# Two half-width units at the front, an interleaved end, and a second per-sample sum on the activation engine

## The chip, the cores and the metric

The kernel runs on one core of one Trainium2 chip. The core has a matrix engine (PE, its weight loads shown apart as PEld), a vector engine (DVE), an activation engine (ACT), a general engine (POOL), and a queue engine (SP) that mostly issues transfers. Sixteen DMA engines move the data. The metric is the device time of one execution in microseconds (us); lower is better. A "profiled execution" is one run recorded by the hardware profiler; its rows are what is read here.

## The reference

A recommendation model's interaction tower, 1024 samples, 32 embedding fields of 16 numbers, three interaction layers of 64 outputs, then a dense tower:

```python
B, M, D, LAYERS = 1024, 32, 16, [64, 64, 64]
e = jnp.stack([tbl_f[ids[:, f]] for f in range(32)], axis=1)      # (B, M, D)
x0 = e; xk = x0; outs = []
for W in (W0, W1, W2):                                            # (M, h, 64)
    xk = relu(einsum('bmd,bhd,mhk->bkd', x0, xk, W))
    outs.append(sum(xk, axis=2))                                  # over d
z = concatenate(outs, axis=1)                                     # (B, 192)
h = concatenate([z, dense_ctx], axis=1)                           # (B, 208)
h = maximum(h @ W_top1 + b_top1, 0)                               # 512
h = maximum(h @ W_top2 + b_top2, 0)                               # 256
y = h @ W_top3                                                    # (B, 1)
```

Everything is 32-bit float. Per sample and per d, a layer is the outer product of the 32 fields with the layer's input, contracted with a weight matrix. The sum over d of each layer's output is what "the sums" mean below.

## The kernel before

**Units.** The samples are worked on in 16 units of 64. The free axis of a tile holds one unit's samples and d values, N = 64 x 16 = 1024 columns, in two halves (blk) of 512. Layers 2 and 3 contract 32 x 64 = 2048 pairs, 16 tiles of 128 partitions; layer 1 uses symmetry and takes 4 tiles and one small tile of squares.

**How a unit gets its data.** POOL gathers the rows of a unit from the tables with 16 indirect transfers (line 295), 64 samples times two groups of fields on 128 partitions. DVE transposes them (`turn`, line 331) into xt, 8 transfers (`store`, line 205) write them to a scratch tensor in HBM three times over, and SP loads them back spread over partitions: `first` (line 226, 0.5 MB, for x0) and four groups of four tiles (`load_group`, line 231, 2 MB each) into a ring of 6 buffers.

**What computes.** DVE multiplies tiles by the layer's input (x0, x1 or x2, in PSUM) into prod, a ring of 12 tiles (`multiply`, line 341), in steps of 1, 2 or 4 tiles. POOL makes 3 of 16 tiles of layers 2 and 3 (tiles 5, 6, 7; line 307) from copies x1_pool and x2_pool. PE contracts each tile with its weights, one matmul for each half of the columns, into the PSUM bank acc (`contract`, line 484; a matmul shows as two records in the profile, so a tile is four records). ACT evicts acc with a relu into x1 or x2 (line 392, four pieces), into the POOL copy (four more), and into relu_out (`keep`, line 407), from which the sum over d is taken into z.

**The sums.** For layers 1 and 2 DVE takes one reduction (`sum_d`, line 353). For layer 3 ACT does it (`sum_3`, line 400): 32 small activations with an accumulator output, each recorded as an ACTIVATE and a READ_ACCUMULATOR.

**Order.** Nothing is scheduled by a tool; each engine's list is written by hand and the semaphores tie them together. PE takes layer 2 of unit u, layer 1 of u+1, layer 3 of u. DVE takes the same order; inside layer 3 of u it sums layer 2 after step 2 and turns unit u+2 before step 3, and after layer 3 it sums layer 1 of u+1. ACT's list per unit: x0 of u+1 (`base_tile`, line 413), squares of u+1 (line 419), x2 of u (`after_2`), x1 of u+1 (`after_1`), relu_out of layer 3 of u (`after_3`), its sum. SP's list: the stores of u+1, `first`, groups 0 and 1, then group 2 once DVE made step 0 of layer 3 of u, group 3 once it made step 1 and POOL its third tile.

**The end.** For the last unit there is no next layer 1 to put between layer 2 and layer 3. Then the dense tower runs for all samples at once, 512 columns per matmul (lines 542 and 546 for the first matrix, 553, 559), with ACT evictions (lines 471, 475, 478), and two output transfers (line 285).

## Time and profile before

| | |
|---|---|
| median of 3 runs | 680.73 us (674.42 to 684.67) |
| the profiled execution | 675.9 us, of which 674.0 us is the span of the trace |
| TensorE clock, mean granted | 0.967 of full speed |
| busy: PE, DVE, ACT, POOL | 85%, 83%, 47%, 68% |
| HBM | 227 GB/s mean over the span |

Time stamps are us from the span's start. A row of the timeline reads: start, length, engine, line, operation, written <- read, shapes, count; in brackets the idle time of the engine ahead of it and what ended that. The row of a group merges neighbouring instructions and shows the form of the first.

### The profile page before, as it was taken

The page shows a single profiled execution, that of the slowest core. Times are in us where ns is not written, and L with a number is a line of the kernel's source. Part 1 is how long each engine was busy: PE and PEld are TensorE (multiplying, and loading weights), DVE is VectorE, ACT ScalarE, POOL GpSimd, SP SyncE. Part 2 cuts the span into 40 slices and gives each one's busy share as a digit, 9 for nine tenths or more (in the row PEclk, how much of TensorE's full clock was granted, in tenths as well). Part 3 has the DMA queues.
Part 4 walks back from the last instruction along what each step waited for, and adds up shares of the span by engine and source line. Part 5 has one row for each costly group of instructions (what it writes and reads, how often), then busy time and mean ns, then how long its engine had stood idle before and what let it go on. Part 6 is the DMA issues. An engine that isn't in the chain of part 4 may idle for free.

```text
span 674.0 us, 7501 instructions
## 1 busy us (share of the span) xinstructions
PE 572.9 (85%) x2472; PEld 191.5 (28%) x2472; DVE 558.0 (83%) x231; ACT 317.5 (47%) x1311; POOL 461.0 (68%) x353
## 2 busy tenths in 40 slices
PE   0047599989989898989898989898998989895997
PEld 0002132333323232323232323232333423231332
DVE  0039798989999999999899999999998999996400
ACT  0031447364555646454646473746456464643031
POOL 5776484977878887878697979788887873443000
PEclk9998699899999899989999999999898999997999
DMA  3296685776757576767586777777685667570000
GB/s 91 65 353 218 261 300 230 271 286 254 298 223 298 223 248 253 255 256 283 214 301 241 276 282 273 285 270 287 244 311 201 248 241 309 206 243 0 1 0 0
DMA packets 32918, 153.35 MB, mean 228 GB/s; under 512 B 11600, under 2 KB 21584, under 8 KB 24816
## 3 DMA queue, kind: packets, MB, share of 16 engines
q1 hardware_dynamic: 22656, 149.31, 57.6%
q0 software_dynamic: 8192, 2.11, 2.6%
q10 hardware_dynamic: 2032, 1.46, 0.7%
q8 instruction: 19, 0.31, 0.2%
q14 instruction: 19, 0.16, 0.1%
HBM read 147.61 MB, written 5.25 MB: 227 GB/s over the span
## 4 chain that ended last, share of the span: by engine, by line
PE 52%; DVE 21%; DMA 11%; issue 6%; ACT 5%; SPq 3%; POOL 2%; ACTq 0%; DVEq 0%
PE acc L484 47%; DVE prod L341 19%; DMA spread<-x_scratch 6%; DMA x_scratch<-xt 4%; ACT x L392 4%; SPq L205 3%; POOL rows L295 2%; PE x L553 2%; PE x L542 1%; DVE z L353 1%; DVE xt L331 1%; DMA first<-x_scratch 1%; PE x L559 1%; PE x L546 0%; PE acc L542 0%
## 5 line engine op out<-in xcount | busy, mean ns | idle before, releaser
L341 DVE TENSOR_TENSOR prod<-spread,x 128x4096 f32<-128x4096 f32 (+2 forms) x179 | 531.1, 3022 | 47.7 <-ACT x L392 20.4
L484 PE MATMUL acc<-prod,w 128*64 128x512 f32 x1932 | 453.7, 617 | 95.1 <-DVE prod L341 89.5
L295 POOL DMA_INDIRECT rows<-table,idx x256 | 242.7, 948 | 79.0 <-issue 70.4
L307 POOL TENSOR_TENSOR prod_pool<-spread,x_pool 128x1024 f32<-128x1024 f32 x93 | 218.1, 2374 | 84.3 <-ACT x_pool L392 84.1
L484 PEld LDWEIGHTS acc<-prod,w 128*64 128x64 f32 x1932 | 147.8, 141 | 389.5 <-issue 351.7
L392 ACT ACTIVATE x<-acc 64x512 f32<-64x512 f32 x128 | 73.0, 570 | 79.0 <-PE acc L484 77.8
L407 ACT ACTIVATE relu_out<-acc 128x512 f32<-128x512 f32 x48 | 28.7, 597 | 157.3 <-PE acc L484 156.5
L400 ACT ACTIVATE relu_out<-relu_out 128x16 f32<-128x16 f32 x480 | 95.3, 200 | 0.5
L484 PE MATMUL acc<-prod_pool,w 128*64 128x512 f32 x372 | 90.9, 592 | 0.0
L400 ACT ACTIVATION_READ_ACCUMULATOR relu_out<-relu_out 128x1 f32 x480 | 89.8, 187 | 0.0
L392 ACT ACTIVATE x_pool<-acc 64x512 f32<-64x512 f32 x128 | 75.7, 591 | 1.9
L484 PEld LDWEIGHTS acc<-prod_pool,w 128*64 128x64 f32 x372 | 28.4, 137 | 51.4 <-issue 49.7
L419 ACT ACTIVATE square<-spread 32x1024 f32<-32x1024 f32 x16 | 16.9, 1056 | 39.7 <-DMA spread<-x_scratch 39.7
L353 DVE TENSOR_REDUCE z<-relu_out 128x32 f32<-128x512 f32 x33 | 22.2, 674 | 5.8 <-ACT relu_out L407 5.8
L413 ACT ACTIVATE x<-first 128x1024 f32<-128x1024 f32 x16 | 16.4, 1028 | 20.3 <-DMA first<-x_scratch 19.9
L331 DVE STREAM_TRANSPOSE xt<-rows 128x256 f32<-128x256 f32 x16 | 10.6, 661 | 15.1 <-DMA rows<-table,idx 15.1
L484 PE MATMUL acc<-square,w_sq 32*64 32x512 f32 x64 | 17.2, 613 | 0.0
L553 PE MATMUL x<-prod,spread 128*128 128x512 f32 x32 | 14.0, 594 | 0.9 <-ACT prod L471 0.9
L413 ACT ACT_TABLE_LOAD x1 | 1.3, 1283 | 28.3 <-issue 28.3
L542 PE MATMUL x<-z,spread 64*128 64x512 f32 x36 | 8.5, 606 | 1.5 <-DVE z L353 1.5
L553 PEld LDWEIGHTS x<-prod,spread 128*128 128x128 f32 x32 | 6.0, 190 | 8.8 <-issue 8.8
L471 ACT ACTIVATE prod<-x,b 128x512 f32<-128x512 f32 x6 | 3.8, 683 | 9.9 <-PE x L546 9.9
(20 smaller groups left out, 26.9 us busy)
## 6 DMA issues: line engine op xcount, KB each, us to landing
spread<-x_scratch SPq DMA_DIRECT2D x63, 2048.0 KB, 9.3
first<-x_scratch SPq DMA_DIRECT2D x16, 512.0 KB
rows<-table,idx POOLq DMA_INDIRECT x256
x_scratch<-xt SPq DMA_DIRECT2D x64, 48.0 KB
spread<-x_scratch SPq DMA_DIRECT2D x4, 512.0 KB, 8.2
x_scratch<-xt SPq DMA_DIRECT2D x60, 32.0 KB
w<-w ACTq DMA_DIRECT2D x2, 512.0 KB, 5.7
spread<-wt SPq DMA_DIRECT2D x2, 384.0 KB, 4.4
```

Source lines behind the costliest of these rows:

```text
L205: engine.dma_start(to, src.to_broadcast([J, times, BLK // 2])).then_inc(scratch_in[u % 2], 16)
L295: nc.gpsimd.indirect_dma_start(rows[u % 2][:, j * D:(j + 1) * D], None, table, bass.IndirectOffsetOnAxis(ap=idx[:, u, j:j + 1], axis=0)).t ...
L307: nc.gpsimd.tensor_tensor(prod_pool[:, k % POOL_SLOTS, :], tiles(u, t, 1)[:, 0, :], x[:, :], ALU.mult).then_inc(pool_ready, 1)
L331: nc.vector.transpose(xt[u % 2][:, :].rearrange("p (b e) -> p e b", e=D // 2), rows[u % 2][:, :].rearrange("p (j e c) -> p e c j", e=D // ...
L341: nc.vector.tensor_tensor(prod[:, at:at + count, :], tiles(u, t, count), x[:, :].rearrange("p (a n) -> p a n", a=1).to_broadcast([P, count ...
L353: nc.vector.tensor_reduce(z[:, layer, u * 32:(u + 1) * 32], relu_out[layer][:, :].rearrange("p (e b d) -> p b e d", e=2, d=D // 2), axis=m ...
L392: last = nc.scalar.activation(to[K * half:K * half + K, blk * BLK:(blk + 1) * BLK], src[K * blk:K * blk + K, :], ACT.Relu)
L400: last = nc.scalar.activation(kept[:, b, :, :], kept[:, b, :, :], ACT.Copy, accum_out=z[:, 2, u * 32 + b:u * 32 + b + 1])
L407: nc.scalar.activation(relu_out[layer][:, :], src[:, :], ACT.Relu).then_inc(relu_ready[layer], 1)
L413: nc.scalar.activation(x0[:, :], first[:, :], ACT.Copy).then_inc(x0_ready, 1)
L484: last = nc.tensor.matmul(to[K * blk:K * blk + K, :], w, moving[:, blk * BLK:(blk + 1) * BLK], start=start, stop=stop)
L553: last = nc.tensor.matmul(to_h2(t, g), w_top2[:, s, t * P:(t + 1) * P], h_1[:, s, g, :], start=s == 0, stop=s == H1 // P - 1)
```

## The change

Four edits come together.

1. **Half units.** The first 64 samples are worked on as two units of 32 (u = 0 and 1), each with half as many columns (512) and with its rows on four groups of fields, so that 8 indirect transfers gather a unit. Then come 15 units of 64; in all there are 17 units, and the last has the number LAST = 16. A half unit's scratch is written by 10 transfers of its own (`store_half`), half of them by ACT for unit 0. Layer 3 of unit 0 and layer 2 of unit 1 are all made by DVE. The ids come laid out by the host, in two transfers. An activation on one element (`warm`) is placed ahead of ACT's first wait on the transposed rows.
2. **Interleaved end.** Of layer 3 of unit 15, steps 0 and 1 and the POOL tiles are taken first, then layer 2 of unit 16, then the rest of layer 3 of unit 15, then layer 3 of unit 16, whose input x2 is written to the place of x0. PSUM banks come from a table (BANKS).
3. **Sums of layer 1.** From unit 1 on ACT makes them with the 32 small activations, right after `after_1`; DVE keeps that of unit 0 alone.
4. **Tower.** The 64 samples of the half units have z of 128 partitions (the two halves of d) instead of 64, so the first matrix takes 480 columns in the old way and 2 x 32 columns in matmuls of their own. There are four output transfers.

```diff
+HALVES = 2
+UNITS = HALVES + (B - HALVES * S // 2) // S
+LAST = UNITS - 1
+FULL = (UNITS - HALVES) * S // 2
+COLS = FULL + HALVES * S // 2
...
-    return () if (layer, u) == (2, 0) else (5, 6, 7)
+    return () if (layer, u) in ((2, 0), (3, 0), (2, 1)) else (5, 6, 7)
...
+CUT = 2
+CUT_ORDER = ([("step", 0), ("step", 1), ("pool", 0), ("pool", 1), ("pool", 2)], [("step", 2), ("step", 3)])
+
+
+def sequence():
+
+    def every(layer, u):
+        return [(layer, u, i) for i in range(len(steps_of(layer, u)))]
+
+    yield from every(1, 0)
+    for u in range(LAST):
+        yield from every(2, u)
+        yield from every(1, u + 1)
+        if u + 1 < LAST:
+            yield from every(3, u)
+    yield from every(3, LAST - 1)[:CUT]
+    yield from every(2, LAST)
+    yield from every(3, LAST - 1)[CUT:]
+    yield from every(3, LAST)
...
+        def store_half(engine, u, f):
+            for copy in range(copies(u, f)):
+                to = scratch(u, J // 2 * f + M * copy)
+                to = bass.AP(tensor=to.tensor, offset=to.offset, ap=[[N // 8, 4], [N // 2, J // 2], [1, N // 8]])
+                engine.dma_start(to, xt[u % 2][32 * f:32 * f + 32, 0:N // 8]).then_inc(scratch_in[u % 2], 16)
...
             turn(0)
             layer_1(0)
-            for u in range(UNITS):
+            turn(1)
+            for u in range(LAST):
                 dve.wait_ge(x_ready[0], u + 1)
                 for i in range(len(steps_of(2, u))):
                     multiply(2, u, i, x1)
-                    if u == 0 and i == 2:
-                        turn(1)
                 if u == 0:
                     sum_d(0, 0)
-                if u + 1 < UNITS:
-                    layer_1(u + 1)
+                layer_1(u + 1)
                 dve.wait_ge(x_ready[1], u + 1)
-                for i in range(len(steps_of(3, u))):
-                    if i == 3 and u + 2 < UNITS:
-                        turn(u + 2)
-                    multiply(3, u, i, x2)
-                    if i == 2:
-                        sum_d(u, 1)
-                if u + 1 < UNITS:
-                    sum_d(u + 1, 0)
-            sum_d(UNITS - 1, 2)
+                if u + 1 < LAST:
+                    for i in range(len(steps_of(3, u))):
+                        if i == (1 if u == 0 else 3) and u + 2 < UNITS:
+                            turn(u + 2)
+                        multiply(3, u, i, x2)
+                        if i == 2:
+                            sum_d(u, 1)
+            for i in range(CUT):
+                multiply(3, LAST - 1, i, x2)
+            sum_d(LAST - 1, 1)
+            dve.wait_ge(x_ready[0], LAST + 1)
+            for i in range(len(steps_of(2, LAST))):
+                multiply(2, LAST, i, x1)
+            for i in range(CUT, len(steps_of(3, LAST - 1))):
+                multiply(3, LAST - 1, i, x2)
+            dve.wait_ge(x_ready[1], LAST + 1)
+            for i in range(len(steps_of(3, LAST))):
+                multiply(3, LAST, i, x2_of(LAST))
+                if i == 1:
+                    sum_d(LAST, 1)
+            sum_d(LAST, 2)
...
-            def sum_3(u):
-                act.wait_ge(relu_ready[2], u + 1)
-                kept = relu_out[2][:, :].rearrange("p (e b d) -> p b e d", e=2, d=D // 2)
+            def sum_d(u, layer):
+                act.wait_ge(relu_ready[layer], u + 1)
+                kept = relu_out[layer][:, 0:width(u) // 2].rearrange("p (c b e) -> p b c e", c=2, b=S // 2)
                 for b in range(S // 2):
                     last = nc.scalar.activation(kept[:, b, :, :], kept[:, b, :, :], ACT.Copy,
-                                                accum_out=z[:, 2, u * 32 + b:u * 32 + b + 1])
-                last.then_inc(summed[2], 1)
+                                                accum_out=z[:, layer, z_at(u) + b:z_at(u) + b + 1])
+                last.then_inc(summed[layer], 1)
...
+            act.wait_ge(consts_in, 48)
+            nc.scalar.activation(warm[:, :], w_sq[0:1, 0:1], ACT.Relu)
             act.wait_ge(turned, 1)
-            store(act, 0, 1)
+            for f in range(1, 4, 2):
+                store_half(act, 0, f)
             base_tile(0)
             squares(0)
             after_1(0)
-            for u in range(UNITS):
-                if u + 1 < UNITS:
-                    base_tile(u + 1)
-                    if u:
-                        squares(u + 1)
+            for u in range(LAST):
+                base_tile(u + 1)
+                if u:
+                    squares(u + 1)
                 after_2(u)
-                if u + 1 < UNITS:
-                    after_1(u + 1)
-                after_3(u)
-                if u + 1 < UNITS:
-                    sum_3(u)
+                after_1(u + 1)
+                sum_d(u + 1, 0)
+                if u + 1 < LAST:
+                    after_3(u)
+                    sum_d(u, 2)
+            after_2(LAST)
+            after_3(LAST - 1)
+            sum_d(LAST - 1, 2)
+            after_3(LAST)
...
+            for u in range(LAST):
+                layer(u, 2, order_of(2, u))
+                layer_1(u + 1)
+                if u + 1 < LAST:
+                    layer(u, 3, order_of(3, u))
+            done = layer(LAST - 1, 3, CUT_ORDER[0])
+            layer(LAST, 2, order_of(2, LAST))
+            layer(LAST - 1, 3, CUT_ORDER[1], done)
+            layer(LAST, 3, order_of(3, LAST))
...
-                        nc.tensor.matmul(to_h1(t, g), w_top1[own, l, t * P:(t + 1) * P], z[own, l, :],
-                                         start=l == 0, stop=False)
+                        nc.tensor.matmul(to_h1(t, g)[:, 0:FULL], w_top1[own, l, t * P:(t + 1) * P],
+                                         z[own, l, 0:FULL], start=l == 0, stop=False)
                 for g in range(2):
                     own = slice(64 * g, 64 * g + D)
-                    nc.tensor.matmul(to_h1(t, g), w_dense[own, t * P:(t + 1) * P], dense[own, :],
+                    nc.tensor.matmul(to_h1(t, g)[:, 0:FULL], w_dense[own, t * P:(t + 1) * P], dense[own, 0:FULL],
+                                     start=False, stop=True)
+
+                for g in range(HALVES):
+                    for l in range(3):
+                        nc.tensor.matmul(to_h1(t, g)[:, FULL:BLK], w_top1[:, l, t * P:(t + 1) * P],
+                                         z[:, l, z_at(g):z_at(g) + S // 2], start=l == 0, stop=False)
+                    own = slice(64 * g, 64 * g + D)
+                    nc.tensor.matmul(to_h1(t, g)[:, FULL:BLK], w_dense[own, t * P:(t + 1) * P], dense[own, FULL:BLK],
                                      start=False, stop=True).then_inc(h1_mm, 1)
```

ACT, in the steady stretch, one unit from the activations x0 of u+1 to those of the next. Before:

```order
L413 ACTIVATE x<-first 128x1024
L419 ACTIVATE square<-spread 32x1024
L392 ACTIVATE x<-acc 64x512 x4
L392 ACTIVATE x_pool<-acc 64x512 x4
L407 ACTIVATE relu_out<-acc 128x512
L392 ACTIVATE x<-acc 64x512 x4
L392 ACTIVATE x_pool<-acc 64x512 x4
L407 ACTIVATE relu_out<-acc 128x512 x2
L400 ACTIVATE relu_out,z<-relu_out 128x2x8 x32
```

The changed kernel, the same stretch (L528 is x0, L534 squares, L506 the evictions, L522 relu_out, L514 the sums):

```order
L528 ACTIVATE x<-first 128x1024
L534 ACTIVATE square<-spread 32x1024
L506 ACTIVATE x<-acc 64x512 x4
L506 ACTIVATE x_pool<-acc 64x512 x4
L522 ACTIVATE relu_out<-acc 128x512
L506 ACTIVATE x<-acc 64x512 x4
L506 ACTIVATE x_pool<-acc 64x512 x4
L522 ACTIVATE relu_out<-acc 128x512
L514 ACTIVATE relu_out,z<-relu_out 128x2x8 x32
L522 ACTIVATE relu_out<-acc 128x512
L514 ACTIVATE relu_out,z<-relu_out 128x2x8 x32
```

The two relu_out of one row (layer 1 of u+1, then layer 3 of u) now have 32 summing activations between them.

DVE at the end, from layer 3 of the last unit but one on. Before (L353 are the sums, L341 the products):

```order
L341 TENSOR_TENSOR prod<-spread,x 128x1024
L341 TENSOR_TENSOR prod<-spread,x 128x4096
L353 TENSOR_REDUCE z<-relu_out 128x32
L341 TENSOR_TENSOR prod<-spread,x 128x4096
L353 TENSOR_REDUCE z<-relu_out 128x32
L341 TENSOR_TENSOR prod<-spread,x 128x2048 x2
L341 TENSOR_TENSOR prod<-spread,x 128x1024
L341 TENSOR_TENSOR prod<-spread,x 128x4096
L341 TENSOR_TENSOR prod<-spread,x 128x2048 x2
L341 TENSOR_TENSOR prod<-spread,x 128x4096
L341 TENSOR_TENSOR prod<-spread,x 128x1024
L341 TENSOR_TENSOR prod<-spread,x 128x4096
```

The changed kernel (L452 the sums, L439 the products):

```order
L439 TENSOR_TENSOR prod<-spread,x 128x1024
L452 TENSOR_REDUCE z<-relu_out 128x32
L439 TENSOR_TENSOR prod<-spread,x 128x2048 x2
L439 TENSOR_TENSOR prod<-spread,x 128x1024
L439 TENSOR_TENSOR prod<-spread,x 128x4096
L439 TENSOR_TENSOR prod<-spread,x 128x2048 x2
L439 TENSOR_TENSOR prod<-spread,x 128x4096 x3
L439 TENSOR_TENSOR prod<-spread,x 128x1024
L452 TENSOR_REDUCE z<-relu_out 128x32
L439 TENSOR_TENSOR prod<-spread,x 128x4096 x2
L452 TENSOR_REDUCE z<-relu_out 128x32
```

Between the last layer 2 (2, 2, 1, 4, 2, 2 tiles) and the first step of the last layer 3 there now stand the two steps of 4 tiles that are left of the layer 3 before it; the row "x3" is those two and that first step.

PE in the tower, one of the four output tiles of the first matrix. Before, and then the changed kernel:

```order
L542 MATMUL x<-z,spread 128x512 x6
L546 MATMUL x<-spread 128x512 x2
```

```order
L669 MATMUL x<-z,spread 128x480 x6
L673 MATMUL x<-spread 128x480 x2
L678 MATMUL x<-z,spread 128x32 x3
L681 MATMUL x<-spread 128x32
L678 MATMUL x<-z,spread 128x32 x3
L681 MATMUL x<-spread 128x32
```

Eight matmuls of 32 columns follow the eight long ones, each with a weight load of 128 columns.

## Rows read from the trace of the kernel before

**Rows 1.** The page: the span in 40 slices, busy tenths of DVE.

```profile
DVE  0039798989999999999899999999998999996400
```

**Rows 2.** The chain that ended last, one unit that closes through PE (start, length, what).

```profile
363.75 0.57 ACT x L392
...
377.15 4.26 DVE prod L341
381.46 17.56 PE acc L484 x80
399.05 0.57 ACT x L392
```

**Rows 3.** The timeline of DVE, one unit that closes through the transfers.

```profile
304.59 0.66 DVE L331 STREAM_TRANSPOSE xt<-rows 128x256 f32<-128x256 f32 x1
...
326.14 4.42 DVE L341 TENSOR_TENSOR prod<-spread,x 128x4096 f32<-128x4096 f32 x1 [1.80 <-issue]
...
341.19 0.66 DVE L331 STREAM_TRANSPOSE xt<-rows 128x256 f32<-128x256 f32 x1
```

**Rows 4.** The chain: the eviction of x2 of unit 1 and of unit 15.

```profile
112.62 0.57 ACT x L392
...
612.75 0.57 ACT x L392
```

**Rows 5.** The timeline of ACT, without the 32 sums at 315.35 to 321.8.

```profile
314.72 0.60 ACT L407 ACTIVATE relu_out<-acc 128x512 f32<-128x512 f32 x1 [8.52 <-PE acc L484]
321.82 1.03 ACT L413 ACTIVATE x<-first 128x1024 f32<-128x1024 f32 x1
326.08 1.06 ACT L419 ACTIVATE square<-spread 32x1024 f32<-32x1024 f32 x1 [3.24 <-DMA spread<-x_scratch]
```

**Rows 6.** Groups by line and form: busy, mean ns of one, idle before.

```profile
L341 DVE TENSOR_TENSOR prod<-spread,x 128x2048 f32<-128x2048 f32 x64 | 143.2, 2277 | 6.1 <-ACT x L392 6.1
L400 ACT ACTIVATE relu_out<-relu_out 128x16 f32<-128x16 f32 x480 | 95.3, 200 | 0.5
L353 DVE TENSOR_REDUCE z<-relu_out 128x32 f32<-128x512 f32 x33 | 22.2, 674 | 5.8 <-ACT relu_out L407 5.8
```

**Rows 7.** The timeline of the start: the last gather of unit 0, and two turns.

```profile
23.44 0.94 POOL L295 DMA_INDIRECT rows<-table,idx  x1 [0.30 <-issue]
...
25.79 0.66 DVE L331 STREAM_TRANSPOSE xt<-rows 128x256 f32<-128x256 f32 x1 [15.15 <-DMA rows<-table,idx]
...
58.09 0.66 DVE L331 STREAM_TRANSPOSE xt<-rows 128x256 f32<-128x256 f32 x1
```

**Rows 8.** The chain, unit 1: layer 1, then PE until x2.

```profile
72.91 4.43 DVE prod L341
77.38 35.21 PE acc L484 x148
...
114.97 4.43 DVE prod L341
```

**Rows 9.** The timeline of DVE and PE at the end.

```profile
595.62 14.33 DVE L341 TENSOR_TENSOR prod<-spread,x 128x2048 f32<-128x2048 f32 x6
615.10 9.88 DVE L341 TENSOR_TENSOR prod<-spread,x 128x4096 f32<-128x4096 f32 x3 [5.14 <-ACT x L392]
...
619.66 5.95 PE L484 MATMUL acc<-prod,w 128*64 128x512 f32 x20 [6.96 <-DVE prod L341]
...
635.09 0.60 ACT L407 ACTIVATE relu_out<-acc 128x512 f32<-128x512 f32 x1 [16.98 <-PE acc L484]
```

**Rows 10.** Groups by line and form: weight loads of the tower.

```profile
L553 PEld LDWEIGHTS x<-prod,spread 128*128 128x128 f32 x32 | 6.0, 190 | 8.8 <-issue 8.8
L559 PEld LDWEIGHTS x<-prod,w_top 128*1 128x1 f32 x8 | 0.6, 83 | 2.8 <-issue 2.8
```

**Rows 11.** The timeline of the tower: first matmuls, and the output transfers.

```profile
636.55 2.85 PE L542 MATMUL x<-z,spread 64*128 64x512 f32 x12 [1.50 <-DVE z L353]
...
670.96 1.24 SPq L285 DMA_DIRECT2D y_out_dram<-prod  x2
```

More of the change, by code:

```diff
@@ L92, in made, with banks @@
+def banks():
+    order = [(1, 0)]
+    for u in range(LAST):
+        order += [(2, u), (1, u + 1), (3, u)]
+    order += [(2, LAST), (3, LAST)]
+    out, had = {}, {}
+    for n, stage in enumerate(order):
+        bank = out[2, LAST][0] if stage == (3, LAST) else n % 2
+        out[stage] = bank, had.get(bank)
+        had[bank] = stage
+    return out
+PLACES, POOL_PLACES, BANKS = places(), pool_places(), banks()
 def made(layer, u, i=-1):
@@ L183, in build, with gathers_done, stores_done @@
         y_mm, y_out, stored = sem("y_mm"), sem("y_out"), sem("stored")
+        def gathers_done(u):
+            return 16 * sum(fields(v) for v in range(u % 2, u + 1, 2))
+        def stores_done(u):
+            return 16 * sum(stores(v) for v in range(u % 2, u + 1, 2))
         def tiles(u, t, n):
```

325 lines of the change are left out of this document (178 added, 147 removed).

## The prediction

> **What bounds the kernel now.** I read the 40 slices first: from the fifth slice to the 36th DVE is at seven tenths at least and mostly at nine or more [rows 1], which looks like an engine that is the bound. The chain of waits says otherwise. In one kind of unit the loop closes through PE: x2 is evicted at 363.75, DVE makes layer 3 until 377.15 + 4.26, PE works 17.56 us without a break on the last 4 tiles of layer 3 and the 16 of the next layer 2, and the next x2 begins at 399.05: 35.3 us [rows 2]. The sum of layer 1 is not on it, as DVE takes it behind its last step of layer 3, while PE has 20 tiles before it. In the other kind the loop closes through the transfers: DVE turns unit u+2 at 304.59, its scratch is written and read, DVE stands idle for 1.80 us until group 0 has landed, starts layer 1 at 326.14 and comes to the next turn at 341.19: 36.6 us [rows 3]. That sum is not on this path either: what it frees, DVE waits longer. The mean over 14 units, from x2 of unit 1 to that of unit 15, is (612.75 - 112.62) / 14 = 35.72 us [rows 4], between the two. So the middle has little to give to edit 3; the start (first turn at 25.79) and the end are where work is missing.
>
> My sums are made against the profiled execution: 675.9 us, 1.9 of them outside its span of 674.0. The median of the runs stands 4.8 us above it, and the lowest run 1.5 below.
>
> **Sums of layer 1: DVE to ACT.** Removed from DVE are 15 reductions of 0.674 us [rows 6]; they overlap their neighbours a little, so some 0.6 us per unit comes free. ACT gets 32 activations for each. The busy rows (200 ns and as much again for the accumulator) would make 12 us, but the two overlap: between the relu_out at 314.72 (0.60 long) and x0 at 321.82 lie 6.5 us for all 32 [rows 5]. They go into the gap ahead of relu_out of layer 3, which is 8.52 us here [rows 5]; it holds them with 2 us to spare, so the added cost is nothing. If this cover were gone, x0 would be late: behind it ACT waits another 3.24 us for the transfer before the squares. The gain goes by rows 2 and 3: nothing in a unit that closes through transfers; in one that closes through PE, PE's 17.56 us hold 80 records. The tower's first 12 took 2.85 [rows 11], so the pace without fill and waits is (17.56 - 2.85) / 68 = 0.216 us a record, 17.3 of the 17.56 are work, and at most 0.3 is to be had. Over 13 units I take 0.1 each, **-1.3 us**, between 0 and 13 x 0.6 = 7.8, the end at which DVE itself were the bound. The Trainium skill speaks against this edit: "ScalarE: Activation LUTs", under "Rules for kernel authors", sends relu, max, min, add and mul to VectorE. The price per sum agrees with it here (6.5 us against 0.67), and were ACT the bound, the edit would cost 15 x 5.8 = 87 us; the row with 8.52 us of idle time decides for me that it costs nothing.
>
> **Half units at the start.** A gather takes 0.94 us and 0.30 to the next [rows 7], so 8 fewer bring the first turn from 25.79 to 15.8. A half tile costs about half on DVE (2277 ns for 2 tiles, 1.1 us each [rows 6]). Two later events decide what is kept.
> First, unit 2, whose samples were the second half of unit 1. Its gathers still end with the 32nd of all, so its turn can't come before about 45.8, 20 us after the 16th's [rows 7]; before, the turn came at 58.09, and layer 1 began 14.2 us after its end, at 72.91 [rows 7, 8]. The turn of unit 2 stands behind layer 1 of unit 1 and one step of layer 3 of unit 0. Working forward from the first turn (loads of half the bytes, x1 at about 30, layer 2 of unit 0 done at 39, unit 1's group 0 landed behind the loads of unit 0 at about 44) I get 48.5. Then 14.2 us as in that quiet start, or 20.9 as in rows 3: layer 1 of unit 2 starts at 63.5 to 70, say 67. ACT holds it there too: before x0 of unit 2 it now has two sums of 6.5 us in the time of a half unit, which don't shrink with it (32 samples each), and is free at about 65.
> Second, x2 of unit 2, which stands where x2 of unit 1 stood, at 112.62: 14 whole units follow both. PE took 35.21 us for 37 tiles [rows 8]; now it has 21 whole and 16 half tiles, 29 in all: 67 + 4.4 + 35.21 x 29 / 37 = 99. But ACT is late again: the sum of layer 1 of unit 2 ends at 91, that of layer 3 of unit 1 at 98, then come x0 and the squares of unit 3, and x2 of unit 2 is out at 102.6; layer 1 of unit 3 runs on DVE from 99 to 103.5. Layer 3 of unit 2 thus starts at 103.6, against 114.97 [rows 8]: **-11 us**. Ends: -17, if unit 2 is turned at 45.8 and its data land in 14.2 us; -5, if also layer 1 of unit 3 waits for transfers of 20.9 us behind a late turn.
>
> **Interleaved end.** Before, DVE ended layer 2 of unit 15 at 609.95, waited until 615.10 for x2, and PE stood still for 6.96 us and ended just before 635.09 [rows 9]. In the new order, counted from the x2 before it (577.96 + 2.35): DVE has 5 + 13 + 8 + 13 tiles and a sum, 43.5 us at 1.1, so it ends at 624 to 625; the eviction of x2 now falls while 8 tiles of the old layer 3 are made. PE has 5 + 8 + 16 + 8 + 16 = 53 tiles; it waits for POOL's third tile and the last steps, and I come to 628.4. **-6.7 us**, between -5 and -7.5. Late next is PE behind DVE's last step of 4 tiles.
>
> **Tower.** 64 samples need 8 matmuls of 32 columns for each of 4 outputs, 32 matmuls or 64 records, each with a load of 128 weight columns. Nothing so short is in the trace. A load takes 190 ns for 128 columns and 83 for one [rows 10], so 107 ns for the columns. From below, loads follow each other: 64 x 0.107 = 6.8. From above, each load in full and then its 27 ns of columns (32 / 512 of 0.43 us, which a full record lasts, as two of 0.216 run beside each other): 64 x 0.217 = 13.9. I take the columns of both in turn, 0.134: 8.6, nearer the lower end because the loads of L553 run under the matmul before them. The long ones shrink from 512 to 480 columns: 64 records x 0.216 x 32 / 512 = 0.9 less. So **+7.7 us**, between +5.9 and +13.0, all on the path, since only ACT works beside it. By the Trainium skill, "TensorE: Matmul & The Clock Gate", "Back-to-back issue gap", a pair of load and matmul of 128 columns takes about 81 ns; by an estimate from that, 64 would take 5.2, and the term would be +4.3. No row here shows such a stream. Two more output transfers: two took 1.24 us to issue [rows 11]: **+1.2 us**.
>
> The early table load, the two transfers for the ids and the bank table cost nothing: the first two lie beside the gathers, the last changes no wait of the middle. The 17th unit adds no columns.
>
> **Sum:** -11 - 1.3 - 6.7 + 7.7 + 1.2 = -10.1, 665.8 us on the profiled run. The same step from the median is 670.6; I take 668, the middle, since it isn't known on which side the next runs fall.
>
> **Rivals.**
> A start that comes whole: unit 2 turned at 45.8, its data quick, loads of weights fully hidden: -17 - 2 - 6.7 + 5.9 + 1.2 = -18.6, 657 us (662 from the median). For it: the loads of the first two units have half the bytes. Against: SP holds the stores of unit 2 back until step 1 of layer 3 of unit 0, and the two sums on ACT.
> Dear small matmuls and a short start: -7 - 0 - 5 + 13.0 + 1.2 = +2, 678 us. For it: loads of all 128 rows can't run beside each other as those of two row groups can.
> Slower: every unit closes through the transfers. If DVE reaches layer 1 earlier it only waits, and the half units bring the middle into step with the late kind: 13 units at up to 36.7 in place of 35.72 make +12.7 in place of the -1.3, in all +3.9, 680 us, 685 from the median. It decides itself where group 0 lands later than 19.3 us after the turn, the DVE work between. Against: the unit of rows 2 took 35.3, and the mean was 35.72.
> The gap on ACT fails: were a sum 12 us long, relu_out of layer 3 and x0 would be 3.5 us late, 0.5 us of it past the landing of group 0: 13 x 0.5 = 6.5, so -3.6, 672 us. Against: 6.5 us is measured.
>
> **Chances.** Forecast 0.48; whole start 0.25; dear matmuls 0.12; all through transfers 0.10; gap fails 0.05. A measurement can tell about 2% (13.5 us here) from no change. Faster by more takes most of the whole start and a tenth of the forecast's spread: 0.30; slower by more only the tails of the two cases above zero: 0.05; within, 0.65. The range takes the whole start nearly whole and the cases above zero but for their tails: 652 to 681.
>
> **What would show it.** First turn near 16, that of unit 2 near 48; layer 3 of unit 2 near 104; 35.3 to 36.6 per unit after that, with DVE's waits for x2 or group 0 longer by 0.6; no ACT sum ahead of a late x2 past unit 3; no DVE gap over 1 us between the last layer 2 and layer 3; PE's last layer ended 50 us after the start of x2 of unit 15; the tower's first matrix 7 to 8 us longer. Units of 34.8 us in the middle would mean that DVE was the bound, and the forecast too high by 10.

## The result, and the profile after

The changed kernel takes 691.0 us (median of 4 runs, 686.4 to 694.0) against 681.0 for the kernel before (4 runs beside it, 674.4 to 684.7): a ratio of 1.018, with a 95% interval of 1.013 to 1.024. It is slower, and my forecast of 668 us with its range up to 681 is wrong, in its sign too. The profiled execution of the changed kernel took 694.0 us, with a span of 691.8 against 674.0 before: +17.8 us. That is more than the 10.0 between the medians, since one profile is of the slowest of four runs and the other, of the kernel before, of a quick one. In all that follows medians are of all runs, ratios with their intervals leave out runs over 1.5% above the quickest of their kernel, and the profiles of e2 and e8 are of runs left out by this.

The 17.8 us are accounted for in four stretches, each cut at events that both traces have.

**Start.** The timeline of DVE, changed kernel: two turns, layer 1 of units 1 and 2, and layer 1 of unit 3 with layer 3 of unit 2 behind it.

```profile
14.65 0.42 DVE L428 STREAM_TRANSPOSE xt<-rows 128x128 f32<-128x128 f32 x1 [9.87 <-DMA rows<-table,idx]
...
48.38 4.48 DVE L439 TENSOR_TENSOR prod<-spread,x 128x2048 f32<-128x2048 f32 x2 [6.83 <-issue]
52.78 0.66 DVE L428 STREAM_TRANSPOSE xt<-rows 128x256 f32<-128x256 f32 x1
...
72.99 9.41 DVE L439 TENSOR_TENSOR prod<-spread,x 128x4096 f32<-128x4096 f32 x4 [3.79 <-ACT x L528]
...
105.99 14.21 DVE L439 TENSOR_TENSOR prod<-spread,x 128x4096 f32<-128x4096 f32 x4 [3.30 <-issue]
```

The first turn is 11.1 us earlier than in [rows 7], more than was forecast. But layer 1 of unit 2 begins at 72.99, and layer 1 of unit 1 began at 72.91 in [rows 8]: of 11.1 us nothing is left at that point. The gain that remains comes later, from the half tiles: layer 3 of unit 2 begins one step of layer 1 after 105.99, at 110.33, against 114.97 [rows 8]. That is -4.6 us where -11 was forecast.

**Middle.** Layer 3 of unit 15 begins at 583.21 (row below). From 110.33 it took 472.9 us for 13 units; before, it was 465.3, from 114.97 to 580.30, where the last layer 3 but one begins. +7.6 us (7.55 unrounded), where -1.3 was forecast. The timeline of DVE, kernel before:

```profile
580.30 9.88 DVE L341 TENSOR_TENSOR prod<-spread,x 128x4096 f32<-128x4096 f32 x3 [0.81 <-ACT x L392]
```

**End.** The timeline of DVE, then of ACT, changed kernel.

```profile
583.21 5.55 DVE L439 TENSOR_TENSOR prod<-spread,x 128x4096 f32<-128x4096 f32 x2 [1.25 <-ACT x L506]
...
601.50 18.61 DVE L439 TENSOR_TENSOR prod<-spread,x 128x2048 f32<-128x2048 f32 x6 [2.10 <-DMA spread<-x_scratch]
```

```profile
633.12 0.60 ACT L522 ACTIVATE relu_out<-acc 128x512 f32<-128x512 f32 x1 [7.63 <-PE acc L607]
```

DVE no longer waits 5.14 us for x2 [rows 9]; what it waits for is 2.10 us inside the last layer 2, for a transfer. From layer 3 of unit 15 to the last relu_out: 49.9 us, against 54.8 before (580.30 to 635.09 [rows 9]). -4.9 us; -6.7 was forecast.

**Tower.** From the last relu_out to the end of the span: 691.8 - 633.1 = 58.7 us, against 674.0 - 635.1 = 38.9. **+19.8 us**, where +7.7 and +1.2 were forecast. This alone is more than the whole difference. The timeline of PE: the second matrix in the kernel before, then the changed kernel, the first output tile (its second eight short records, alike, left out), the long group of the second and of the fourth, and the second matrix.

```profile
652.82 13.97 PE L553 MATMUL x<-prod,spread 128*128 128x512 f32 x32 [0.86 <-ACT prod L471]
```

```profile
634.58 2.69 PE L669 MATMUL x<-z,spread 64*128 64x480 f32 x12 [1.50 <-DVE z L452]
637.19 1.07 PE L673 MATMUL x<-spread 16*128 16x480 f32 x4
638.20 0.85 PE L678 MATMUL x<-z,spread 128*128 128x32 f32 x6
638.98 0.41 PE L681 MATMUL x<-spread 16*128 16x32 f32 x2
...
640.43 4.25 PE L669 MATMUL x<-z,spread 64*128 64x480 f32 x12
...
655.74 5.17 PE L669 MATMUL acc<-z,spread 64*128 64x480 f32 x12
...
666.70 16.68 PE L688 MATMUL x<-prod,spread 128*128 128x512 f32 x32
```

Two things are to be read here. The 16 short records of a tile last from 638.20 to 640.43, 2.23 us or 0.139 each; four tiles make 8.9, less 0.9 for the shorter long ones, so 8.0 us by these rows, close to the forecast's 7.7. But the same 12 long records (L669) take 2.69 us in the first tile, 4.25 in the second and 5.17 in the last, and the 32 records of the next matrix 16.68, where they took 13.97 before. The windows show what goes with it: start:end, length, busy time and count of PE, weight loads, DVE, ACT and POOL, then the granted clock (the last two figures are of the DMA). First the kernel before, then the changed one.

```profile
635.00:652.00 17.00, 15.46 (x66) 5.64 (x64) 0.69 (x1) 4.40 (x8) 0.00 (x0) 1.00 0.00 1
652.00:673.00 21.00, 17.50 (x40) 6.58 (x40) 0.00 (x0) 5.17 (x8) 0.00 (x0) 1.00 0.00 0
```

```profile
634.00:650.00 16.00, 15.42 (x70) 8.51 (x72) 0.43 (x1) 2.75 (x4) 0.00 (x0) 0.84 0.00 0
650.00:666.00 16.00, 16.00 (x58) 8.77 (x54) 0.00 (x0) 2.06 (x3) 0.00 (x0) 0.61 0.00 1
666.00:691.00 25.00, 20.91 (x43) 8.19 (x43) 0.00 (x0) 4.61 (x7) 0.00 (x0) 0.84 0.00 0
```

Before, the clock was at its full level (2.4 GHz) through all of PE's work in the tower. Now it is 0.84, 0.61 and 0.84: the trace has two levels, 1 and 0.5, and the low one (1.2 GHz) was granted from 641.4 to 644.8, from 648.2 to 651.7 and from 655.1 to 672.1: 23.9 us of the 52.3 between PE's first and last matmul of the tower. (The windows' means make 25.6; 1.8 of these lie behind the last matmul, where PE stands idle.) Ahead of the first fall PE had done one tile's long and short matmuls at the full clock. What is left of the 19.8 when 8.0 for the short matmuls and 1.2 for the outputs are taken off is 10.6 us, and it lies where the clock is low: 7.9 in the first matrix and 2.7 in the second.

Two facts on the measure are needed below. The kernel before spread over 672.7 to 689.1 us in 52 runs, on four occasions with medians of 681.0, 682.8, 682.4 and 679.2; the profiled 675.9 us against which I made my sum is from its quick end. And the interval of a ratio is 0.9 to 1.4% wide with ten or more runs of the new kernel, and up to 4.7% with four.

### The profile page after: what moved, and what is told of

Read it like the earlier page. It is cut to its first block, busy times and chain, and to the rows that moved or that the text cites. A ratio compares the mean times of both kernels' runs of the same rounds, so it can differ in the third digit from the quotient of the medians.

```text
span 691.8 us, 9069 instructions
## 1 busy us (share of the span) xinstructions
PE 594.3 (86%) x2684; PEld 217.6 (31%) x2684; DVE 552.2 (80%) x230; ACT 429.9 (62%) x2421; POOL 457.6 (66%) x353
## 4 chain that ended last, share of the span: by engine, by line
PE 51%; DVE 17%; DMA 10%; issue 9%; ACT 8%; SPq 2%; POOL 2%; ACTq 0%; POOLq 0%; DVEq 0%
PE acc L607 43%; DVE prod L439 17%; DMA spread<-x_scratch 5%; ACT relu_out L514 4%; ACT x L506 3%; PE x L688 2%; DMA x_scratch<-xt 2%; PE x L669 2%; POOL prod_pool L400 1%; DMA x_scratch_half<-xt 1%; POOL rows L387 1%; SPq L295 1%; SPq L284 1%; PE acc L669 1%; PE x L678 1%
## 5 line engine op out<-in xcount | busy, mean ns | idle before, releaser
L439 DVE TENSOR_TENSOR prod<-spread,x 128x4096 f32<-128x4096 f32 (+3 forms) x190 | 532.9, 2864 | 64.2 <-issue 31.3
L607 PE MATMUL acc<-prod,w 128*64 128x512 f32 (+1 forms) x2076 | 457.1, 588 | 91.1 <-DVE prod L439 91.0
L400 POOL TENSOR_TENSOR prod_pool<-spread,x_pool 128x1024 f32<-128x1024 f32 (+1 forms) x93 | 214.7, 2339 | 86.0 <-ACT x_pool L506 85.8
L514 ACT ACTIVATE relu_out<-relu_out 128x16 f32<-128x16 f32 (+1 forms) x1024 | 202.7, 200 | 1.0
L514 ACT ACTIVATION_READ_ACCUMULATOR relu_out<-relu_out 128x1 f32 x1024 | 191.6, 187 | 0.0
L506 ACT ACTIVATE x<-acc 64x512 f32<-64x512 f32 (+1 forms) x136 | 74.1, 545 | 80.2 <-PE acc L607 79.0
L607 PE MATMUL acc<-prod_pool,w 128*64 128x512 f32 (+1 forms) x372 | 89.5, 586 | 0.0
L506 ACT ACTIVATE x_pool<-acc 64x512 f32<-64x512 f32 (+1 forms) x136 | 77.0, 566 | 2.0
L522 ACT ACTIVATE relu_out<-acc 128x512 f32<-128x512 f32 (+1 forms) x51 | 29.1, 571 | 51.5 <-PE acc L607 50.7
L534 ACT ACTIVATE square<-spread 32x1024 f32<-32x1024 f32 (+1 forms) x17 | 17.1, 1006 | 46.4 <-DMA spread<-x_scratch 42.9
L607 PEld LDWEIGHTS acc<-prod_pool,w 128*64 128x64 f32 x372 | 28.7, 137 | 49.8 <-issue 48.9
L528 ACT ACTIVATE x<-first 128x1024 f32<-128x1024 f32 (+1 forms) x17 | 16.6, 978 | 26.8 <-DMA first<-x_scratch_half 26.4
L607 PE MATMUL acc<-square,w_sq 32*64 32x512 f32 (+1 forms) x68 | 17.8, 600 | 0.0
L452 DVE TENSOR_REDUCE z<-relu_out 128x32 f32<-128x512 f32 (+1 forms) x19 | 12.1, 636 | 4.4 <-ACT relu_out L522 4.4
L669 PE MATMUL x<-z,spread 64*128 64x480 f32 x36 | 11.3, 776 | 1.5 <-DVE z L452 1.5
```

The lines of the kernel that those rows point to most:

```text
L400: nc.gpsimd.tensor_tensor(prod_pool[:, k % POOL_SLOTS, 0:width(u)], tiles(u, t, 1)[:, 0, :], x[:, 0:width(u)], ALU.mult).then_inc(pool_rea ...
L439: nc.vector.tensor_tensor(prod[:, at:at + count, 0:n], tiles(u, t, count), x[:, 0:n].rearrange("p (a n) -> p a n", a=1).to_broadcast([P, c ...
L452: nc.vector.tensor_reduce(z[:, layer, z_at(u):z_at(u) + S // 2], relu_out[layer][:, 0:n].rearrange("p (c b e) -> p b c e", c=2, b=S // 2), ...
L506: last = nc.scalar.activation(to[K * side:K * side + K, blk * n:(blk + 1) * n], src[K * blk:K * blk + K, 0:n], ACT.Relu)
L514: last = nc.scalar.activation(kept[:, b, :, :], kept[:, b, :, :], ACT.Copy, accum_out=z[:, layer, z_at(u) + b:z_at(u) + b + 1])
L522: nc.scalar.activation(relu_out[layer][:, 0:n], src[:, 0:n], ACT.Relu).then_inc(relu_ready[layer], 1)
```

## The experiments

Three reasons for the loss stood against each other. The short matmuls carry it, in part by their work and in part by the clock behind them: then it goes when they go (e3), and comes when they are put into the kernel before (e5). The sums of layer 1 on ACT slow the start and the middle: then e1 is slower than the kernel before, and e2 quicker than the changed one. The half units slow the middle: then the interleaved end alone (e4) gains and the changed kernel without its short matmuls (e3) doesn't.

### e1_sums_act_alone: the kernel before, with only the sums of layer 1 on ACT

```diff
-                if u + 1 < UNITS:
-                    sum_d(u + 1, 0)
...
                 if u + 1 < UNITS:
                     after_1(u + 1)
+                    sum_act(u + 1, 0)
                 after_3(u)
```

> The kernel before with edit 3 alone: the sums of layer 1 from unit 1 on are made by ACT behind its eviction of x1, nothing else changes. Theory A (the sums are hidden in ACT's gap and only loosen DVE): within 1 us of before per profile, a unit of the middle stays at 35.7 to 35.8 us. Theory B (the sums are what lengthens the middle of the changed kernel from 35.8 to 36.4 us a unit, by making x0 or x2 late): 14 x 0.6 = 8 us slower than before, and ACT stands ahead of x0 or x2 in the chain.

Measured: 684.1 us (4 runs) against 682.8, ratio 1.011 (0.993 to 1.029). No change that can be told, though the interval is wide. Its middle took 472.9 us, like that of kernels with these sums on DVE (472.0 to 472.5, below).

### e2_after_sums_dve: the changed kernel, with these sums back on DVE

```diff
                         if i == 2:
                             sum_d(u, 1)
+                    sum_d(u + 1, 0)
...
                 after_1(u + 1)
-                sum_d(u + 1, 0)
```

> The changed kernel with edit 3 undone: DVE sums layer 1 again, behind layer 3 (for the last unit behind its layer 2). Theory A (the two sums on ACT hold back x0 and x2 only in the half units and unit 2): layer 3 of unit 2 starts 4 to 7 us earlier (104 instead of 110.4), the middle as it was, in all 4 to 7 us faster than the changed kernel. Theory B (they also lengthen the middle): the middle comes back to 35.8, 11 to 15 us faster. Rival (the start is held by transfers alone): 0 to 1 us.

Measured: 689.7 us (683.5 to 698.3, 4 runs), ratio 1.016 (0.992 to 1.039); the changed kernel had 691.0. The start is the telling part. Here is ACT of the changed kernel (x0 of unit 2 and the squares), then ACT and DVE of this one.

```profile
71.36 1.03 ACT L528 ACTIVATE x<-first 128x1024 f32<-128x1024 f32 x1
72.94 1.05 ACT L534 ACTIVATE square<-spread 32x1024 f32<-32x1024 f32 x1 [0.55 <-DMA spread<-x_scratch]
```

```profile
68.22 1.03 ACT L530 ACTIVATE x<-first 128x1024 f32<-128x1024 f32 x1
72.56 1.05 ACT L536 ACTIVATE square<-spread 32x1024 f32<-32x1024 f32 x1 [3.31 <-DMA spread<-x_scratch]
...
72.62 9.42 DVE L439 TENSOR_TENSOR prod<-spread,x 128x4096 f32<-128x4096 f32 x4 [3.87 <-issue]
```

Without the sums x0 is ready 3.1 us earlier, and DVE starts layer 1 at 72.62 in place of 72.99: the transfer of group 0 lands then, and it is the other half of a double wait. In neither kernel can a cost or gain of the sums on ACT be told.

### e3_after_no_small: the changed kernel without its 32 short matmuls

It leaves out the first matrix of the tower for the 64 samples of the half units.

```diff
                                      start=False, stop=True).then_inc(h1_mm, 1)
-                for g in range(HALVES):
-                    for l in range(3):
-                        nc.tensor.matmul(to_h1(t, g)[:, FULL:BLK], w_top1[:, l, t * P:(t + 1) * P],
-                                         z[:, l, z_at(g):z_at(g) + S // 2], start=l == 0, stop=False)
...
```

> The changed kernel without the 32 matmuls of 32 columns in the tower, so the results of the 64 samples of the half units are left out; everything else stays, four output transfers too. If the short matmuls also bring down TensorE's clock behind them: 9.0 us of their own time (8 x 1.12) and about 10 us of clock less, 19 us in all, the tower's clock at 1.00. If the clock falls for another reason (the matmuls of 480 columns, the end before it): 9 us less and the clock still near 0.6 from 650 to 666.

Measured: 676.0 us (668.7 to 678.9, 10 runs), ratio 0.994 (0.987 to 1.001), 15.0 below the changed kernel. The last relu_out on ACT, and windows of its tower:

```profile
633.58 0.60 ACT L522 ACTIVATE relu_out<-acc 128x512 f32<-128x512 f32 x1 [7.64 <-PE acc L607]
```

```profile
634.00:650.00 16.00, 14.55 (x64) 5.65 (x64) 0.69 (x1) 4.35 (x8) 0.00 (x0) 1.00 0.00 0
650.00:671.00 21.00, 17.50 (x40) 6.58 (x40) 0.00 (x0) 4.80 (x8) 0.00 (x0) 0.98 0.00 0
```

The clock stands at 1.00 and 0.98, the latter because it falls at 670.0, behind PE's last matmul (667.9). The tower takes 39.3 us in place of 58.7: 19.4 us less, for 8.9 us of work. The first reason holds as far as this: with the short matmuls the loss of clock goes too. Its middle took 473.1 us from x2 to x2 over 13 units, as in the changed kernel (474.0), so the middle's part is not theirs.

### e4_interleaved_alone: the kernel before, with only the interleaved end

```diff
-    for u in range(UNITS):
-        yield 2, u
...
+    yield from every(3, LAST - 1)[:CUT]
+    yield from every(2, LAST)
+    yield from every(3, LAST - 1)[CUT:]
+    yield from every(3, LAST)
```

> The kernel before with the interleaved end alone (16 units of 64, DVE's sums, the tower as it was). If the end is worth what the two traces say: from the start of layer 3 of the last unit but one to the end of PE's last layer 49 to 50 us instead of 54.8, 5 us faster than before. If its gain in the changed kernel hangs on the half units or on the sums: less than 2 us.

Measured: 676.5 us (671.7 to 679.5, 10 runs) against 682.8, ratio 0.998 (0.993 to 1.003). The timelines of DVE and ACT: layer 3 of unit 15 and the last relu_out.

```profile
582.77 5.55 DVE L377 TENSOR_TENSOR prod<-spread,x 128x4096 f32<-128x4096 f32 x2 [0.81 <-ACT x L441]
...
632.77 0.60 ACT L456 ACTIVATE relu_out<-acc 128x512 f32<-128x512 f32 x1 [7.64 <-PE acc L535]
```

The last relu_out begins at 632.77, 50.0 us after 582.77, against 54.8 before: in the profile the interleaved end is worth 4.8 us by itself, as in the changed kernel. In the times it is not shown: the medians lie 6.3 apart, but the ratio says 0.2%, and its interval does not exclude zero.

### e5_before_short_zeros, e10_short_real, e9_short_last: the short matmuls put into the kernel before

The three have the tower of the kernel before with 512 columns, and 32 short matmuls more. In the first two these stand between the long ones with z and the dense ones; their moving operand is a tile of zeros in the first and real columns of z and of the dense input in the second (whose output for those columns is then another sum). In the third the operand is zeros, and the short ones end each tile, as in the changed kernel.

```diff
+                for g in range(2):
+                    for l in range(3):
+                        nc.tensor.matmul(to_h1(t, g)[:, 480:512], w_top1[:, l, t * P:(t + 1) * P], zero[:, :],
+                                         start=False, stop=False)
+                    own = slice(64 * g, 64 * g + D)
+                    nc.tensor.matmul(to_h1(t, g)[:, 480:512], w_dense[own, t * P:(t + 1) * P], zero[own, :],
+                                     start=False, stop=False)
```

> The kernel before with 32 short matmuls added to its tower: for each of the four outputs eight matmuls of 32 columns with the real weights and a moving operand of zeros, which adds nothing to the result. If short matmuls alone cost their time and the clock behind them: tower (from the last relu_out on) 39.0 + 9.0 + 6 to 11 us, a granted clock under 0.9 there. If they only cost their own time: 48 us, clock 1.00. If the clock fell for something else in the changed kernel (four transfers, 480 columns), also 48.

> The kernel before with the 32 short matmuls in the middle, but with real moving operands (columns 480 to 512 of z and of dense) instead of zeros, so that the outputs of those columns are wrong. If the operand's values matter to the clock: tower 55 to 59 us and the clock down. If not: 48 to 50 us, as with zeros.

> The kernel before with the same 32 short matmuls of zeros, now last of each output's matmuls, as the changed kernel has them, instead of ahead of the two dense ones. If their place is what brings the clock down in the changed kernel's tower: tower 55 to 59 us instead of 48.9, clock near 0.6 in a stretch of it, 8 us slower than with the short ones in the middle. If not: 48 to 50 us.

Measured: 690.6 (e5, 4 runs, 682.4 beside it, ratio 1.015, 1.005 to 1.026); 696.7 (e10, 679.2 beside it, 1.031, 1.026 to 1.035); 694.8 (e9, the same 679.2, 1.021, 1.013 to 1.029). So 8 to 18 us in medians for 8.9 us of work, in a kernel with no half unit. In the profiles the tower took 48.9, 48.9 and 51.9 us against 38.9, so +10.0, +10.0 and +13.0. For e9 this counts from the last relu_out to the end of the span of 693.8:

```profile
641.84 0.60 ACT L410 ACTIVATE relu_out<-acc 128x512 f32<-128x512 f32 x1 [17.82 <-PE acc L487]
```

In e5 and e10 the short matmuls thus cost their work and 1.1 us more, far from the 6 to 11 that were expected; the low clock shows in one group of long matmuls, 4.53 us in place of 2.85. e9 lost 4.1, between its two expectations. The stretch in which the clock fell, of e5, then all of e9's from 634 on, then the group with the low clock, of e5 and of e9:

```profile
650.00:669.00 19.00, 19.00 (x96) 10.64 (x96) 0.00 (x0) 3.80 (x6) 0.00 (x0) 0.91 0.00 0
```

```profile
634.00:650.00 16.00, 14.50 (x74) 6.51 (x72) 2.49 (x2) 1.80 (x3) 0.00 (x0) 1.00 0.00 1
650.00:669.00 19.00, 19.00 (x84) 9.63 (x80) 0.00 (x0) 2.92 (x5) 0.00 (x0) 0.82 0.00 0
669.00:690.00 21.00, 21.00 (x54) 8.81 (x53) 0.00 (x0) 4.71 (x7) 0.00 (x0) 0.92 0.00 1
```

```profile
662.25 4.53 PE L546 MATMUL acc<-z,spread 64*128 64x512 f32 x12
```

```profile
661.92 5.49 PE L546 MATMUL acc<-z,spread 64*128 64x512 f32 x12
```

e10's window of 650 to 669 has 0.91 as well, so in the profiled tower the values of the operand made no difference. In the times they may: e10's ratio is 1.031 and e5's 1.015. e10's profile is of its quickest run (mean granted clock 0.963 over the run; the other three had 0.945 to 0.955), so it does not show what these lost; this stays open. Nor is it shown that the place matters: put last, the short ones took 3.0 us more in one profile, but in the runs e9 (1.021) is not above e10 (1.031).

The 10.6 us of the changed kernel are not reached in any of the three, and there is a difference ahead of the tower that no run takes away. With the old end PE stands still for 7.0 us in the last layer, and the clock is low for 6.8 us there and back only at 629 to 632 (0.66 over 624 to 634 in e5). In these three it fell in the tower only about 18 us after PE's first matmul there. With the interleaved end the clock was at its full level from 600 to 634 in the changed kernel, and there and in e2 and e12 it fell 5.6 to 6.8 us into the tower. Which of the two, the end or the tower's own form, makes the fall early is open: no run has the interleaved end with short matmuls beside 512 columns.

### e12_after_zero_operand: the changed kernel, short matmuls with zeros

It leaves out the half units' 64 samples, but issues every matmul.

```diff
-                                         z[:, l, z_at(g):z_at(g) + S // 2], start=l == 0, stop=False)
+                                         zero[:, :], start=l == 0, stop=False)
```

> The changed kernel with the moving operands of its short matmuls replaced by zeros (the outputs of the 64 samples of the half units are left at zero sums). If the operand's values matter: tower 50 to 51 us instead of 58.7, the clock at 1.00. If not: 55 to 59 us, clock down as before.

Measured: 693.1 us (689.1 to 695.9, 4 runs) against 679.2, ratio 1.025 (1.021 to 1.030): no better than the changed kernel. The windows of its tower:

```profile
634.00:650.00 16.00, 15.56 (x76) 8.90 (x76) 0.29 (x1) 2.75 (x4) 0.00 (x0) 0.89 0.00 0
650.00:669.00 19.00, 19.00 (x67) 10.17 (x64) 0.00 (x0) 3.44 (x5) 0.00 (x0) 0.73 0.00 1
```

The tower took 53.9 us (58.7 in the changed kernel, 55.6 in e2, with the same real operands in both). It lies between the two expectations. Less 38.9, 8.0 and 1.2, the clock took 5.8 us here, 10.6 in the changed kernel and 7.5 in e2: it differs from one execution to the next, and zeros lie at its lower end. e9 lost 4.1 so counted. Why the changed kernel's tower loses 1.7 us more than that at the least stays open; the differences left are the interleaved end ahead of it, 480 columns in place of 512, and groups of accumulation of their own for the short ones.

### e6_fold: no short matmuls, the half units' z folded by one matmul

One matmul of 192 columns with [I I; I I] as its weights adds the two halves of z for the 64 samples, ahead of the last layer 3, where PE waits for DVE anyway; two copies on ACT bring the sums into z, and the tower is the old one with 512 columns.

```diff
+            nc.tensor.matmul(x2[:, 0:192].rearrange("p (l n) -> p l n", l=3), fold[:, :], z[:, :, FULL:COLS],
+                             start=True, stop=True).then_inc(folded, 1)
             layer(LAST, 3, order_of(3, LAST))
...
+                        nc.tensor.matmul(to_h1(t, g), w_top1[own, l, t * P:(t + 1) * P],
+                                         z[own, l, 0:BLK], start=l == 0, stop=False)
```

> The changed kernel with the short matmuls mended: one matmul with a constant matrix of four unit matrices adds the two partition halves of the sums of the half units (192 columns), in PE's list ahead of the last layer 3, and two activations write them into z, so the tower takes 512 columns again as before. Theory (the short matmuls are what made the changed kernel slower): tower 40.2 us instead of 58.7, 18 us faster than the changed kernel, 673 to 677 as a median. If the single matmul or the two activations land on the path of the end: 2 to 4 us of that are lost.

Measured: 671.5 us (669.9 to 683.5, 5 runs) against 682.4, ratio 0.988 (0.980 to 0.995), the quickest version of the study and 19.5 us below the changed kernel, with all its work done. The timeline of PE:

```profile
616.42 0.59 PE L672 MATMUL x<-z,fold 128*128 128x192 f32 x2
617.26 4.51 PE L616 MATMUL acc<-prod,w 128*64 128x512 f32 x20 [0.24 <-DVE prod L441]
```

The fold takes 0.59 us and PE still waits 0.24 us for DVE behind it, so it is free. Of the 32 short matmuls nothing had to be on the path. The clock stands at 1.00 in every window from 600 us on.

### e7_fold_early_turn, e8_fold_early_sums_dve: what the start could give

e7 is e6 with the turn of unit 2 ahead of layer 1 of unit 1, and its stores ahead of the loads of groups 2 and 3 of unit 1. e8 is e7 with the sums of layer 1 on DVE, by the edit of e2.

```diff
                 load_group(u + 1, 1)
+                if u == 0:
+                    sp.wait_ge(turned, 3)
+                    store(sp, 2)
...
                 if u == 0:
                     sum_d(0, 0)
+                    turn(2)
                 layer_1(u + 1)
```

> The former with unit 2 turned by DVE ahead of layer 1 of unit 1 (where DVE waits for data anyway) and its stores issued by SP ahead of groups 2 and 3 of unit 1. Theory A (the start is held by the order turn, stores, group 0 of unit 2): stores from 46.5 instead of 56, group 0 landed 6 to 9 us earlier than 72.9. With ACT's two sums in that place x0 of unit 2 still comes only at 71 to 72, so 1 to 2 us faster than the former. Theory B (ACT does not hold it): 5 to 8 us faster.

> The former with the sums of layer 1 on DVE again. If ACT's sums hold x0 of unit 2 once its data come early: layer 1 of unit 2 starts at 66 to 69 instead of 72, 3 to 5 us faster than the former, and the middle as it is. If the sums on ACT are worth their 0.6 us of DVE time a unit: 5 to 8 us slower than the former in the middle. If neither: within 1.5 us.

The queue of SP, changed kernel (start, length of the issues, what):

```profile
28.72 6.87 SPq L284 DMA_DIRECT2D x_scratch_half<-xt  x10
40.93 0.56 SPq L318 DMA_DIRECT2D first<-x_scratch_half  x1
41.54 14.56 SPq L323 DMA_DIRECT2D spread<-x_scratch_half  x4
56.15 3.94 SPq L295 DMA_DIRECT2D x_scratch<-xt  x8
63.04 0.52 SPq L318 DMA_DIRECT2D first<-x_scratch  x1
```

The stores of unit 1 are ten issues of 6.87 us in all, and land 5.3 us behind the last; unit 2 was turned by 53.44, but its stores stand behind the loads of unit 1 in SP's queue until 56.15, and its first load goes out at 63.04. In e7 its stores go out at 48.76. Its first load on SP, then ACT and DVE:

```profile
55.89 0.54 SPq L320 DMA_DIRECT2D first<-x_scratch  x1
```

```profile
72.03 1.03 ACT L534 ACTIVATE x<-first 128x1024 f32<-128x1024 f32 x1
...
73.09 9.41 DVE L444 TENSOR_TENSOR prod<-spread,x 128x4096 f32<-128x4096 f32 x4 [4.21 <-ACT x L534]
```

The loads come 7.2 us earlier and layer 1 of unit 2 does not: ACT reaches x0 only at 72.03, behind its sums. In e8 both waits are gone:

```profile
68.61 1.03 ACT L536 ACTIVATE x<-first 128x1024 f32<-128x1024 f32 x1
...
69.67 9.41 DVE L444 TENSOR_TENSOR prod<-spread,x 128x4096 f32<-128x4096 f32 x4 [0.67 <-ACT x L536]
```

Together with e2 this shows where the forecast's start was lost: two waits, of SP's queue and of ACT, end within a us of each other at 72 to 73, and removing one leaves the other. With both removed layer 1 begins 3.3 us earlier, and x2 of unit 2 comes at 103.8 in place of 106.9. In the total it is not to be found: e7 took 676.9 us (ratio 0.992, 0.988 to 0.997) and e8 675.7 (0.991, 0.986 to 0.995), 11 runs each, both above the 671.5 of e6's 5 runs, with intervals that overlap.

### The middle

Thirteen profiles can be lined up here. From x2 to x2 over the same 13 units, and in brackets the time within it at 1.2 GHz, added up from the trace's records of the granted clock:

```
before 465.3 (20.5)   e4 469.9 (23.9)   e6 471.8 (30.7)   e10 472.0 (27.3)
e9     472.1 (27.3)   e5 472.5 (27.3)   e1 472.9 (30.7)   e3  473.1 (30.7)
e12    473.4 (30.7)   after 474.0 (30.7)   e7 474.4 (34.1)   e2 480.8 (34.1)   e8 481.3 (37.5)
```

e5, e9 and e10 have the code of the kernel before up to the tower, and took 472 us. So the profile that I had of the kernel before was its lowest, and of the changed kernel's +7.6 us (layer 3 to layer 3; 8.6 from x2 to x2) about 6.7 are the spread of the same code. The order goes roughly with the time at the low clock, but these profiles do not show which is cause: a unit that waits longer may also lose its clock.

## Why the prediction was wrong

**The step that failed is the tower's term.** It was put at +7.7 us "between +5.9 and +13.0", with every record timed at the full clock. The work was sized well (8.0; rows of weight loads alone gave it). But behind the short matmuls the granted clock fell to 0.61 in a window of 16 us: 10.6 us more, so the term measured 18.6, beyond the upper end. e3 shows that without them the clock stays at its full level through all of PE's work, e9 that they lower it in a kernel without half units too (4.1 us), e6 that the kernel gains with all its work done and without them. What brings the clock down behind them, and why it costs 1 us in e5 and 6 to 11 in the changed kernel's tower, stays open. I read [rows 10] for the duration of a load and never asked what a stream at 0.14 us a record, with little to compute in each, does to the clock. The rival of the dear small matmuls had the sign and the wrong mechanism: it priced loads that can't overlap, at 0.217 us a record, and the records came every 0.139.

**The start: -4.6 in place of -11.** The first turn was right to 1.2 us, the turn of unit 2 late by 4.3 (52.78 for 48.5), layer 1 of unit 2 by 6.0 (72.99 for 67) and layer 3 of unit 2 by 6.7 (110.33 for 103.6), which lies beyond my weaker end of -5. The loss is a mis-sized wait: unit 1's ten stores and their landing, and its group 0, which DVE got at 48.38 where I had 44. ACT was forecast free at 65 and was at 71.36, since the sums began late in turn.

**The middle: +7.6 in place of -1.3.** The term for the sums on ACT can't be told from zero: in medians they cost 1.3 (e1), 1.3 (e2 undoes them) and 1.2 us (e8 against e7), each less than these runs can tell apart, though all of one sign, and that not mine. What was wrong is the base. The note that the median stood 4.8 us above the profiled run was there, and I took the middle of the two; 52 runs say that the profiled run was a quick one, and the sum should have been made from the median. The rival by which each unit closes through the transfers gave +12.7 for the middle and would seem confirmed; e5, e9 and e10 say that it isn't, as they show the same 472 us with whole units. (Its condition was put at 19.3 us from the turn to group 0; [rows 3] give 19.1.)

**The end: -4.9 in place of -6.7**, 0.1 us beyond my weaker end; the group of the last unit landed 2.10 us late for DVE, and e4's profile gives the same 4.8 by itself. **The outputs** took their 1.2 us. No wait on the old x2 was left, as forecast.

In times it comes to this, as ratios to the kernel before: 1.018 for the changed kernel, 0.994 without its short matmuls (e3) and 0.988 with the fold in their place (e6), so the short matmuls cost 2.4 to 3.0%, or 15.0 to 19.5 us in medians. The interleaved end alone has 0.998 (e4), and e3, which has the half units and ACT's sums besides, 0.994 with an interval that overlaps it: what the end and the half units gained in the profiles, 4.9 and 4.6 us, these times neither show nor exclude.

## What to carry to other kernels

Before short matmuls go on the path, read the granted clock behind the nearest like them, and if there are none, put a term for the clock in the range: here it cost 6 to 11 us beside 8.0 us of work. Where two engines or queues wait for one start, price the second wait before the first is removed. And make a sum from the median of the runs, for a profile of one execution may be its quickest.

## What the hardware showed that was not expected

- 16 short records (32 columns, weights of 128 columns) took 2.23 us, 0.139 each, at the full clock. The Trainium skill, "TensorE: Matmul & The Clock Gate", "Back-to-back issue gap", gives about 81 ns for a pair of load and matmul of 128 columns; for this stream of fp32 the measurement decides against it.
- Before, TensorE was at its full level through all of its work in the tower, and with 8.0 us more work, all in short matmuls, it was at 1.2 GHz for 23.9 of 52.3 us, though it never stood idle. In the middle of each tile they cost about 1 us of clock (two profiles), at its end in the same kernel 4 (one profile), and 6 to 11 in the changed kernel's tower (three profiles). With zeros as operands the changed kernel's ratio was 1.025 against 1.018; in the kernel before it was 1.015 with zeros and 1.031 with real ones, which stays open.
- The same kernel took 672.7 to 689.1 us in 52 runs, with its middle of 13 units between 465.3 and 472.5 us in four profiles of the same code.
